# Second pair of PSUM banks for the odd node blocks at the end of a GNN layer, with task lists of their own

## The chip, the cores and the metric

The kernel runs on one core of a Trainium2 chip. The metric is the device time of one execution in microseconds; the kernel before took 619.28 us, the median of three runs (618.55 to 620.71).

## What is computed

One layer of a graph network over N = 50000 nodes and E = 25000 edges (sorted by destination), with rows of H = 128 floats, in fp32. The reference, cut:

```python
em = jnp.concatenate([x[src], x[dst]], axis=-1)
em = relu(layer_norm(em @ msg_w + msg_b, msg_g, msg_beta)) * edge_weights[:, None]
messages = segment_sum(em, dst) / (counts + 1e-08) * valid
gate = sigmoid(x @ gate_w + gate_b)
combined = jnp.concatenate([x, messages], axis=-1)
h_new = relu(layer_norm(combined @ upd_w + upd_b, upd_g, upd_beta))
out = layernorm(x + gate * h_new + (1.0 - gate) * x)
```

## The kernel before

**Tiling.** The edges come in 49 groups of 512 (four tiles of 128), the nodes in 98 blocks of 512, taken as 49 pairs k = 0 to 48; (k, 0) is the even and (k, 1) the odd block of a pair. P = 128, ROW = 129 (128 columns and one for the gate).

**Walk.** Each engine runs the same numbered steps: some written out, a loop, and from step 48 on written out again. Edge group g is worked on in step g, and the nodes follow a few steps behind it, since a block's messages must be stored first. Each engine has a list of tasks by hand; `node(task, at, lag, b)` runs a task for block (step - lag, b), and skips it where that pair doesn't exist; `edge` does the same for the groups. Engines are tied together by counting semaphores only, and each works its list strictly in order. After step 48 there are no edge groups left but the last `message_update` (L747) in step 49, so steps 49 to 52 (ACT: to 53) hold node tasks alone.

**A node block, in order of its data.** SP loads x_rows (L371) and the window of summed-up message rows (L389). PE transposes x into ps_x (`x_transposes`, L755) and ACT copies it to xT (`xT_of`, L555). DVE builds the one-hot matrix (`one_hots`, L1042). PE forms the sums u = x W + onehot messages in ps_u, two tiles at a time (`first_update`, `other_update`, L765 and L767). ACT takes their squares with row sums (`first_squares`, `other_squares`, L560), the gate (`gates`, L576), log and exp of the variance (`u_ln_of` L581, `u_rstd_of` L586), and then normalises out of ps_u into un (`first_norms`, `other_norms`, L593). PE transposes un into ps_t (`update_transposes`, L782), ACT applies scale, shift and relu (`hT_of`, L606), PE transposes back into ps_h (`back_transposes`, L789). DVE adds the residual (`residual`, L1056), takes statistics (`y_halves`, L1063) and some eight small operations (`sums`, L1073 to L1093), ACT gives log and exp of that variance (`y_ln_of` L611, `y_rstd_of` L616), and DVE writes the rows (`result`, L1108), which SP stores (L404).

**PSUM.** ps_xs and ps_xd are the banks of the edge transposes, ps_z that of the messages; ps_x, ps_t and ps_h one bank each. ps_u has two banks: tiles 0 and 1 of a block in one, 2 and 3 in the other, and every block uses the same two. So `update` waits until the block before has been normed out of the same bank:

```python
wait(pe, un_ready, k.at(4, 2 * b - 1 + a))
```

**The lists before, in the node steps.** With the lag and b in brackets, edge tasks left out. ACT: u_rstd(4,1), xT(3,0), norms(4,1), first squares(3,0), y_ln(5,1), hT(4,1), y_rstd(5,1), other squares(3,0), xT(3,1), gates(3,0), u_ln(3,0), u_rstd(3,0), norms(3,0), y_ln(4,0), y_rstd(4,0), hT(3,0), both squares(3,1), u_ln(3,1), gates(3,1). PE: back(4,0), first update(3,0), update transposes(4,1), other update(3,0), x transposes(3,1), back(4,1), first update(3,1), update transposes(3,0), other update(3,1), x transposes(2,0). DVE: residual(4,1), result(4,0), y_halves(4,1), one_hots(2,0), sums(4,1), residual(3,0), one_hots(2,1), result(4,1), y_halves(3,0), sums(3,0). ACT runs y_rstd of (s - 5, 1) in its step s, for the result that DVE has in its step s - 1. `sums` holds the small operations of the named y and also the first of the gate of the following block.

Of the kernel before, what the change touches and what calls it, by code (L numbers as in the profile page):

```python
# [7 lines left out]
ACT = mybir.ActivationFunctionType  # L8
AX = mybir.AxisListType
F32 = mybir.dt.float32  # L10
# [3 lines left out]
P = 128  # L14
# [12 lines left out]
ROW = P + 1  # L27
# [34 lines left out]
def gnn_kernel(nc, x, src, dst, edge_weight, msg_w, msg_b, msg_g, msg_beta,  # L62
# [8 lines left out]
    NK = NB // 2  # L71
# [10 lines left out]
    with ExitStack() as ctx:  # L82
        def sb(name, shape, dt=F32):
            return ctx.enter_context(nc.sbuf_tensor(name, shape, dt))

        def psum(name):
            return ctx.enter_context(nc.psum_tensor(name, [P, 512], F32))
# [17 lines left out]
        u_x_gate = sb("u_x_gate", [P, ROW])  # L105
# [14 lines left out]
        squares = sb("squares", [P, 3, 512])  # L120
# [10 lines left out]
        xT = [sb(f"xT{s}", [P, 512]) for s in range(2)]  # L131
        onehot = [sb(f"onehot{s}", [P, 512]) for s in range(2)]
# [3 lines left out]
        gate_exp = [sb(f"gate_exp{s}", [P, T]) for s in range(2)]  # L136
        gate_small = [sb(f"gate_small{s}", [P, 3, T]) for s in range(2)]
        un = [sb(f"un{s}", [P, 512]) for s in range(2)]
# [13 lines left out]
        node_recip = sb("node_recip", [P, 3, T])  # L152


        ps_xs = psum("ps_xs")
        ps_xd = psum("ps_xd")
        ps_z = psum("ps_z")
        ps_x = psum("ps_x")
        ps_t = psum("ps_t")
# [1 line left out]
        ps_u = ctx.enter_context(nc.psum_tensor("ps_u", [P, 1024], F32))  # L161
        ps_h = psum("ps_h")

        def sel_out(n):

            return (ps_h, ps_x, ps_t)[n // 3][:, n % 3 * ROW:(n % 3 + 1) * ROW]

        def u_tile(j, n):
            return ps_u[:, (j // 2) * 512 + (j % 2) * ROW:][:, 0:n]

        u_by_bank = ps_u[:].rearrange("p (a c) -> p a c", a=2)[:, :, 0:2 * ROW].rearrange(
            "p a (t h) -> p a t h", h=ROW)
        u_gates = u_by_bank[:, :, :, P:ROW]


        w_mean = sb("w_mean", [P, 4])
# [56 lines left out]
        def walk_sem(name):  # L233
            walk_sems.append(sem(name))
            return walk_sems[-1]
# [21 lines left out]
        hot_ready, un_ready, y_ready, y_var_ready, out_ready = (  # L257
            walk_sem("hot_ready"), walk_sem("un_ready"), walk_sem("y_ready"),
            walk_sem("y_var_ready"), walk_sem("out_ready"))
# [4 lines left out]
        def wait(eng, semaphore, value):  # L264

            if not (isinstance(value, int) and value <= 0):
                eng.wait_ge(semaphore, value)
# [4 lines left out]
        def walk(eng, step, last_lag, unroll=2):  # L272

            count = (NK - 1 - last_lag - 2) // unroll
            start = NK - 1 - unroll * count
            for c in range(start):
                step(Step(c))
            with eng.Fori(0, count) as m:
                for c in range(start, start + unroll):
                    step(Step(c, m, unroll))  # L280
            for c in range(NK - 1, NK + last_lag):
                step(Step(c))

        def edge(task, at, lag):
            g = at.back(lag)
            if g.inside(HEAD, EG):
                task(g)

        def node(task, at, lag, b):
            k = at.back(lag)  # L290
            if k.inside(0, NK):
                task(k, b)
# [30 lines left out]
        def _(sp):  # L323
# [129 lines left out]
            with is_general(sp):  # L453
                for s in range(2):
                    sp.wait_ge(rows_stored[s], 16)
                restart(sp, 1)
                all_edges(sp, store_rows)
                sum_by_node()
                restart(sp, 2)
                head()  # L460
                walk(sp, lambda at: step(at, by_window=False), 4)
            with sp.Else():
                walk(sp, step, 4)
# [43 lines left out]
        def _(act):  # L507
# [49 lines left out]
            def u_squares(k, b, a):  # L557
                act.wait_ge(u_done, k.at(4, 2 * b + a + 1))
                for j in (2 * a, 2 * a + 1):
                    last = nc.scalar.activation(squares[:, b, j * P:(j + 1) * P], u_tile(j, P), ACT.Square,  # L560
                                                accum_out=u_square[b][:, j:j + 1])
                if a == 1:
                    last.then_inc(u_square_ready, 1)
# [7 lines left out]
            def gates(k, b):  # L571
                act.wait_ge(u_done, k.at(4, 2 * b + 2))
                if k.m is None:

                    wait(act, gate_chain, k.at(4, 2 * b - 3))
                nc.scalar.activation(gate_exp[b][:].rearrange("p (a t) -> p a t", a=2).unsqueeze(3), u_gates,  # L576
                                     ACT.Exp, bias=gate_bias[:], scale=-1.0).then_inc(gate_exp_ready, 1)

            def u_ln_of(k, b):
# [8 lines left out]
            def u_norm(k, b, a):  # L588
                if a == 0:
                    act.wait_ge(u_rstd_ready, k.at(2, b + 1))  # L590
                    wait(act, un_in, k.at(2, b - 1))
                for j in (2 * a, 2 * a + 1):
                    last = nc.scalar.activation(un[b][:, j * P:(j + 1) * P], u_tile(j, P), ACT.Copy,  # L593
                                                scale=u_rstd[b][:, j:j + 1])
                last.then_inc(un_ready, 1)

# [31 lines left out]
                    whole_edge(Step(g))  # L628

            def step(at):  # L630
                node(u_rstd_of, at, 4, 1)
                node(xT_of, at, 3, 0)
                node(first_norms, at, 4, 1)
                node(other_norms, at, 4, 1)
                edge(xsT_of, at, 0)
                edge(xdT_of, at, 0)
                node(first_squares, at, 3, 0)
                node(y_ln_of, at, 5, 1)
                node(hT_of, at, 4, 1)
                node(y_rstd_of, at, 5, 1)  # L640
                node(other_squares, at, 3, 0)
                node(xT_of, at, 3, 1)
                node(gates, at, 3, 0)
                node(u_ln_of, at, 3, 0)
                node(u_rstd_of, at, 3, 0)
                node(first_norms, at, 3, 0)
                node(other_norms, at, 3, 0)
                edge(z_squares, at, 0)
                node(y_ln_of, at, 4, 0)
                edge(z_ln_of, at, 0)  # L650
                node(y_rstd_of, at, 4, 0)
                edge(z_rstd_of, at, 0)
                node(hT_of, at, 3, 0)
                node(first_squares, at, 3, 1)
                node(other_squares, at, 3, 1)
                edge(emT_of, at, 0)
                node(u_ln_of, at, 3, 1)
                node(gates, at, 3, 1)
# [14 lines left out]
        def _(pe):  # L673
            def tile(t, j):
                return t[:, j * P:(j + 1) * P]
# [15 lines left out]
            for n in range(2 * T):  # L691
                for c in range(2):
                    last = nc.tensor.matmul(sel_out(n), sel[:, c, n * P:(n + 1) * P], sel_rhs[:, c, :],
                                            start=c == 0, stop=c == 1)
# [63 lines left out]
            def update(k, b, a):  # L758
                slot = 2 * (k.c % 2) + b
                if a == 0:  # L760
                    pe.wait_ge(xT_ready, k.at(2, b + 1))
                    pe.wait_ge(hot_ready, k.at(2, b + 1))
                wait(pe, un_ready, k.at(4, 2 * b - 1 + a))
                for j in (2 * a, 2 * a + 1):
                    nc.tensor.matmul(u_tile(j, ROW), tile(xT[b], j), u_x_gate[:], start=True, stop=False,  # L765
                                     skip_group_check=True)
                    last = nc.tensor.matmul(u_tile(j, P), tile(onehot[b], j),  # L767
                                            window[slot][:, j * ROW:j * ROW + P], start=False, stop=True,
                                            skip_group_check=True)
                last.then_inc(u_done, 1)  # L770
# [48 lines left out]
                    message_update(g)  # L819

            def step(at):
                node(back_transposes, at, 4, 0)
                edge(dst_transposes, at, 0)
                edge(message_update, at, 1)
                edge(src_transposes, at, 0)
                node(first_update, at, 3, 0)
                node(update_transposes, at, 4, 1)
                node(other_update, at, 3, 0)
                node(x_transposes, at, 3, 1)
                edge(message, at, 0)  # L830
                node(back_transposes, at, 4, 1)
                node(first_update, at, 3, 1)
                node(update_transposes, at, 3, 0)
                node(other_update, at, 3, 1)
                node(x_transposes, at, 2, 0)
                edge(message_transposes, at, 0)
# [23 lines left out]
            with is_general(pe):  # L860
                restart(pe, 1)
                for c in range(2):
                    last = nc.tensor.transpose(ps_u[:, c * P:(c + 1) * P], weight_f[:, c, :], ident)
# [379 lines left out]
```

## Time and profile before

| what | value |
|---|---|
| median of 3 runs | 619.28 us (618.55 to 620.71) |
| the profiled execution | 617.63 us, its span 615.8 us |
| busy, share of the span | PE 89%, DVE 86%, ACT 86%, POOL 62% |
| granted TensorE clock, mean | 0.970 of 2.4 GHz |
| last edge work on PE (L747) | 572.08 us |
| last result of DVE begins | 611.94 us |

All times below are of the profiled execution, in us from the start of its span. A row of a timeline gives the start, the duration, the engine, line and operation, and, in brackets, how long the engine stood idle before it and what released it. Durations of one engine's rows can overlap a little: what an instruction takes of its engine is the distance to the next start.

### The profile page before, as it was taken

What the parts mean: (1) busy time and instruction counts of PE and PEld (TensorE: products, weight loads), DVE (VectorE), ACT (ScalarE), POOL (GpSimd) and SP (SyncE); (2) the same over time, 40 slices, a digit from 0 to 9 for tenths busy, and PEclk for the clock granted to TensorE, in tenths of its full rate; (3) what the DMA queues carried; (4) which work ended last, traced back from release to release, by engine and by line L of the source; (5) the groups of instructions that cost most, each with busy time, mean ns of one, the idle gap of its engine ahead of it and who ended that gap; (6) DMA issues with size and microseconds to landing.
All of it is one profiled execution on the core that took longest, in us unless ns stands there. A gap on an engine that the chain in (4) does not pass through costs nothing.

```text
span 615.8 us, 19234 instructions
## 1 busy us (share of the span) xinstructions
PE 546.9 (89%) x4552; PEld 522.8 (85%) x4600; DVE 532.2 (86%) x2434; ACT 531.7 (86%) x2500; POOL 382.5 (62%) x396
## 2 busy tenths in 40 slices
PE   1354799999999999999999999999999999999761
PEld 0353799999999999999999999999999999999660
DVE  4990159999989999999999999999999999999986
ACT  0021499999999999999999999999999999999883
POOL 0787777777777777777776767677676776300000
PEclk9985799999999999999999999999999999999996
DMA  3213468887878878788787877878778787756642
GB/s 108 70 43 91 134 177 212 208 228 203 225 214 212 221 201 229 209 210 224 199 227 200 219 209 212 224 190 225 211 211 220 198 227 198 205 156 169 173 116 69
DMA packets 192823, 115.12 MB, mean 187 GB/s; under 512 B 15053, under 2 KB 186390, under 8 KB 192790
## 3 DMA queue, kind: packets, MB, share of 16 engines
q1 hardware_dynamic: 178550, 88.63, 51.6%
q0 software_dynamic: 12544, 25.72, 18.2%
q10 hardware_dynamic: 1696, 0.40, 0.3%
q8 instruction: 13, 0.21, 0.1%
q14 instruction: 20, 0.16, 0.1%
HBM read 75.72 MB, written 38.97 MB: 186 GB/s over the span
## 4 chain that ended last, share of the span: by engine, by line
PE 70%; ACT 13%; DVE 9%; issue 5%; DMA 2%; SPq 1%; DVEq 0%; ACTq 0%
PE ps_u L765 12%; PE ps_u L767 11%; PE ps_z L747 8%; PE ps_z L732 7%; PE ps_z L734 6%; PE ps_t L782 5%; PE ps_h L789 5%; PE ps_x L755 5%; PE ps_xs L741 4%; ACT squares L560 3%; PE ps_xd L715 3%; PE ps_xs L715 3%; ACT un L593 3%; ACT squares L534 2%; ACT hT L606 1%
## 5 line engine op out<-in xcount | busy, mean ns | idle before, releaser
L471 POOL DMA_INDIRECT pair_rows<-in_x,gather_idx x392 | 382.3, 975 | 146.9 <-issue 112.6
L765 PE MATMUL ps_u<-u_x_gate,xT 128*128 128x129 f32 x784 | 155.2, 280 | 9.5 <-ACT un L593 9.2
L767 PE MATMUL ps_u<-window,onehot 128*128 128x128 f32 x784 | 151.2, 274 | 0.0
L765 PEld LDWEIGHTS ps_u<-u_x_gate,xT 128*128 128x128 f32 x784 | 118.5, 191 | 13.0 <-issue 6.4
L767 PEld LDWEIGHTS ps_u<-window,onehot 128*128 128x128 f32 x784 | 119.0, 192 | 0.0
L1108 DVE TENSOR_SCALAR out_rows<-y,y_small,y_rstd 128x128 f32<-128x128 f32 x392 | 111.6, 359 | 4.5 <-ACT y_rstd L616 4.5
L593 ACT ACTIVATE un<-ps_u,u_rstd 128x128 f32<-128x128 f32 x392 | 112.1, 373 | 3.2
L1056 DVE SCALAR_TENSOR_TENSOR y<-ps_h,gate_small,x_rows 128x128 f32<-128x128 f32 x392 | 109.9, 343 | 1.0 <-PE ps_h L789 1.0
L560 ACT ACTIVATE squares<-ps_u 128x128 f32<-128x128 f32 x392 | 107.6, 300 | 3.5 <-PE ps_u L767 3.3
L560 ACT ACTIVATION_READ_ACCUMULATOR squares<-ps_u 128x1 f32 x392 | 90.1, 232 | 0.0
L1063 DVE BATCH_NORM_STATS2 y_stats<-y 128x6 f32<-128x128 f32 x392 | 84.8, 280 | 0.0
L732 PE MATMUL ps_z<-weights,xsT 128*128 128x128 f32 x392 | 76.9, 278 | 4.6 <-ACT xsT L524 1.6
L606 ACT ACTIVATE hT<-ps_t,columns 128x512 f32<-128x512 f32 x98 | 77.7, 793 | 2.8 <-PE ps_t L782 2.7
L734 PE MATMUL ps_z<-weights,xdT 128*128 128x128 f32 x392 | 77.2, 279 | 0.0
L1042 DVE SCALAR_TENSOR_TENSOR onehot<-window,const_in 128x512 f32<-128x512 f32 x98 | 72.8, 743 | 4.1 <-DMA window<-rows_scratch 3.4
L732 PEld LDWEIGHTS ps_z<-weights,xsT 128*128 128x128 f32 x392 | 64.6, 195 | 1.9
L524 ACT COPY xsT<-ps_xs 128x512 f32<-128x512 f32 x49 | 29.8, 609 | 40.3 <-PE ps_xs L715 40.3
L534 ACT ACTIVATE squares<-ps_z 128x128 f32<-128x128 f32 x196 | 52.2, 304 | 11.1 <-PE ps_z L734 11.1
L747 PE MATMUL ps_z<-weights,emT 128*128 128x128 f32 x392 | 59.1, 296 | 2.7 <-ACT emT L549 2.4
L747 PEld LDWEIGHTS ps_z<-weights,emT 128*128 128x128 f32 x392 | 49.5, 198 | 13.4 <-ACT emT L549 12.4
L734 PEld LDWEIGHTS ps_z<-weights,xdT 128*128 128x128 f32 x392 | 60.8, 196 | 0.0
L782 PE MATMUL ps_t<-const_in,un 128*128 128x128 f32 x392 | 58.9, 273 | 2.0 <-ACT un L593 2.0
(133 smaller groups left out, 1023.3 us busy)
## 6 DMA issues: line engine op xcount, KB each, us to landing
x_rows<-in_x SPq DMA_DIRECT2D x98, 256.0 KB
out<-out_rows SPq DMA_DIRECT2D x98, 256.0 KB
window<-rows_scratch SPq DMA_DIRECT2D x196, 112.9 KB
rows_scratch<-msg_rows SPq DMA_DIRECT2D x49, 258.0 KB
pair_rows<-in_x,gather_idx POOLq DMA_INDIRECT x392
const_in<-in_constants SPq DMA_DIRECT2D x1, 954.0 KB, 5.3
rows_scratch<-pad_rows SPq DMA_DIRECT2D x5, 64.5 KB, 3.0
weights<-in_L_gnn_msg_w ACTq DMA_DIRECT2D x1, 128.0 KB, 5.2
```

The lines of the kernel that those rows point to most:

```text
L471: return nc.gpsimd.indirect_dma_start(rows[:, j * P:(j + 1) * P], None, x, bass.IndirectOffsetOnAxis(ap=offsets, axis=0))
L560: last = nc.scalar.activation(squares[:, b, j * P:(j + 1) * P], u_tile(j, P), ACT.Square, accum_out=u_square[b][:, j:j + 1])
L593: last = nc.scalar.activation(un[b][:, j * P:(j + 1) * P], u_tile(j, P), ACT.Copy, scale=u_rstd[b][:, j:j + 1])
L732: nc.tensor.matmul(tile(ps_z, j), tile(xsT[g.c % 2], j), w_src, start=False, stop=False, skip_group_check=True)
L734: last = nc.tensor.matmul(tile(ps_z, j), tile(xdT[g.c % 2], j), w_dst, start=False, stop=True, skip_group_check=True)
L747: last = nc.tensor.matmul(tile(ps_z, j), tile(emT[g.c % 2], j), u_msg, start=True, stop=True)
L765: nc.tensor.matmul(u_tile(j, ROW), tile(xT[b], j), u_x_gate[:], start=True, stop=False, skip_group_check=True)
L767: last = nc.tensor.matmul(u_tile(j, P), tile(onehot[b], j), window[slot][:, j * ROW:j * ROW + P], start=False, stop=True, skip_group_check ...
L782: last = nc.tensor.transpose(tile(ps_t, j), tile(un[b], j), ident)
L1056: last = v.scalar_tensor_tensor(y[b][:, cols], ps_h[:, cols], gates[:, 1, j:j + 1], x_rows[2 * (k.c % 2) + b][:, cols], ALU.mult, ALU.add)
L1063: last = v.bn_stats(y_stats[b][:, j], y[b][:, j * P:(j + 1) * P])
L1108: last = v.tensor_scalar(out_rows[b][:, cols], y[b][:, cols], y_small[b][:, 5, j:j + 1], y_rstd[b][:, j:j + 1], ALU.subtract, ALU.mult)
```

## The change

ps_xs and ps_xd become two halves of one tensor ps_e (the same two banks in all). In the pairs 46, 47 and 48 the odd block's sums go to ps_e instead of ps_u, and a block then waits for the norms of the block two before it, (46, 1) for none. From step 49 on ACT and PE follow new lists. DVE's, SP's and POOL's lists stay.

```diff
-        ps_xs = psum("ps_xs")
-        ps_xd = psum("ps_xd")
+        ps_e = ctx.enter_context(nc.psum_tensor("ps_e", [P, 1024], F32))
+        ps_xs, ps_xd = ps_e[:, 0:512], ps_e[:, 512:1024]
...
-        def u_tile(j, n):
-            return ps_u[:, (j // 2) * 512 + (j % 2) * ROW:][:, 0:n]
+        def after_edges(k):
+            return k.m is None and k.c >= NK - 3
+
+        def u_banks(k, b):
+            return ps_e if after_edges(k) and b == 1 else ps_u
+
+        def u_tile(k, b, j, n):
+            return u_banks(k, b)[:, (j // 2) * 512 + (j % 2) * ROW:][:, 0:n]
...
+        def all_in(at):
+
+            return at.m is None and at.c >= NK
...
             def step(at):
+                if all_in(at):
+                    node(u_rstd_of, at, 4, 1)
+                    node(first_norms, at, 4, 1)
+                    node(other_norms, at, 4, 1)
+                    node(xT_of, at, 3, 0)
+                    node(first_squares, at, 3, 0)
+                    node(other_squares, at, 3, 0)
+                    node(gates, at, 3, 0)
+                    node(u_ln_of, at, 3, 0)
+                    node(xT_of, at, 3, 1)
+                    node(u_rstd_of, at, 3, 0)
+                    node(hT_of, at, 4, 1)
+                    node(first_norms, at, 3, 0)
+                    node(other_norms, at, 3, 0)
+                    node(y_ln_of, at, 5, 1)
+                    node(y_rstd_of, at, 5, 1)
+                    node(first_squares, at, 3, 1)
+                    node(other_squares, at, 3, 1)
+                    node(hT_of, at, 3, 0)
+                    node(u_ln_of, at, 3, 1)
+                    node(gates, at, 3, 1)
+                    node(y_ln_of, at, 4, 0)
+                    node(y_rstd_of, at, 4, 0)
+                    return
...
-                wait(pe, un_ready, k.at(4, 2 * b - 1 + a))
+                if not after_edges(k) or (k.c, b) == (NK - 3, 0):
+                    wait(pe, un_ready, k.at(4, 2 * b - 1 + a))
+                elif k.c > NK - 3:
+
+                    wait(pe, un_ready, k.at(4, 2 * b - 3 + a))
...
             def step(at):
+                if all_in(at):
+                    node(back_transposes, at, 4, 0)
+                    edge(message_update, at, 1)
+                    node(first_update, at, 3, 0)
+                    node(other_update, at, 3, 0)
+                    node(x_transposes, at, 3, 1)
+                    node(update_transposes, at, 4, 1)
+                    node(first_update, at, 3, 1)
+                    node(other_update, at, 3, 1)
+                    node(back_transposes, at, 4, 1)
+                    node(x_transposes, at, 2, 0)
+                    node(update_transposes, at, 3, 0)
+                    return
```

The first `step` is ACT's, the second PE's; the readers of the sums (squares, gates, norms) take the banks from `u_banks` as well.

## Rows read from the trace of the kernel before

**Rows 1.** Windows: stretch, length, busy of PE, PEld, DVE, ACT, POOL; PEclk, DMA, GB/s

```profile
574.68:584.66 9.98, 6.67 (x58) 6.25 (x57) 9.98 (x51) 8.26 (x38) 0.00 (x0) 1.00 0.67 180
584.66:594.64 9.98, 6.66 (x58) 6.25 (x57) 8.88 (x45) 8.27 (x38) 0.00 (x0) 1.00 0.55 151
```

**Rows 2.** Who waited for whom, 571 to 616 us: us, times, longest

```profile
PE ps_u L765 <- ACT un L593: 8.5, 6, 1.7
...
DVE out_rows L1108 <- ACT y_rstd L616: 4.5, 4, 1.6
```

**Rows 3.** Timeline of PE: start us, us, what, [idle before <- releaser]

```profile
578.45 0.46 PE L765 MATMUL ps_u<-u_x_gate,xT 128*128 128x129 f32 x2 [1.60 <-ACT un L593]
...
579.42 0.60 PE L782 MATMUL ps_t<-const_in,un 128*128 128x128 f32 x4
...
580.75 0.60 PE L755 MATMUL ps_x<-const_in,x_rows 128*128 128x128 f32 x4
581.19 0.60 PE L789 MATMUL ps_h<-const_in,hT 128*128 128x128 f32 x4
```

**Rows 4.** Timeline of ACT, same columns

```profile
572.17 0.20 ACT L586 ACTIVATE u_rstd<-u_ln 128x4 f32<-128x4 f32 x1
572.27 0.58 ACT L555 COPY xT<-ps_x 128x512 f32<-128x512 f32 x1
572.73 1.16 ACT L593 ACTIVATE un<-ps_u,u_rstd 128x128 f32<-128x128 f32 x4
574.68 0.28 ACT L560 ACTIVATE squares<-ps_u 128x128 f32<-128x128 f32 x1 [0.80 <-PE ps_u L767]
...
575.29 0.78 ACT L606 ACTIVATE hT<-ps_t,columns 128x512 f32<-128x512 f32 x1
575.96 0.21 ACT L616 ACTIVATE y_rstd<-y_ln 128x4 f32<-128x4 f32 x1
576.05 0.28 ACT L560 ACTIVATE squares<-ps_u 128x128 f32<-128x128 f32 x1
...
577.17 0.24 ACT L581 ACTIVATE u_ln<-u_square 128x4 f32<-128x4 f32 x1
577.45 0.20 ACT L586 ACTIVATE u_rstd<-u_ln 128x4 f32<-128x4 f32 x1
577.68 1.14 ACT L593 ACTIVATE un<-ps_u,u_rstd 128x128 f32<-128x128 f32 x4
```

**Rows 5.** Timeline of DVE, same columns

```profile
576.41 1.11 DVE L1108 TENSOR_SCALAR out_rows<-y,y_small,y_rstd 128x128 f32<-128x128 f32 x4
...
579.04 1.12 DVE L1056 SCALAR_TENSOR_TENSOR y<-ps_h,gate_small,x_rows 128x128 f32<-128x128 f32 x4
...
581.88 0.73 DVE L1042 SCALAR_TENSOR_TENSOR onehot<-window,const_in 128x512 f32<-128x512 f32 x1
...
586.17 1.12 DVE L1108 TENSOR_SCALAR out_rows<-y,y_small,y_rstd 128x128 f32<-128x128 f32 x4 [1.10 <-ACT y_rstd L616]
...
596.15 1.11 DVE L1108 TENSOR_SCALAR out_rows<-y,y_small,y_rstd 128x128 f32<-128x128 f32 x4 [1.31 <-ACT y_rstd L616]
...
605.13 1.12 DVE L1108 TENSOR_SCALAR out_rows<-y,y_small,y_rstd 128x128 f32<-128x128 f32 x4 [1.56 <-ACT y_rstd L616]
```

**Rows 6.** Timeline of PE, 64 to 65 us and its last two groups

```profile
64.53 0.63 PE L732 MATMUL ps_z<-weights,xsT 128*128 128x128 f32 x2 [1.59 <-ACT xsT L524]
64.95 0.63 PE L734 MATMUL ps_z<-weights,xdT 128*128 128x128 f32 x2
...
603.53 0.66 PE L782 MATMUL ps_t<-const_in,un 128*128 128x128 f32 x4 [2.03 <-ACT un L593]
605.06 0.66 PE L789 MATMUL ps_h<-const_in,hT 128*128 128x128 f32 x4 [0.87 <-ACT hT L606]
```

**Rows 7.** Windows around the last work of PE, columns as in rows 1

```profile
604.00:606.00 2.00, 0.85 (x6) 0.42 (x4) 0.87 (x4) 0.87 (x2) 0.00 (x0) 1.00 0.00 0
606.00:607.00 1.00, 0.00 (x0) 0.00 (x0) 1.00 (x6) 0.00 (x0) 0.00 (x0) 0.71 0.00 0
```

More of the change, by code:

```diff
@@ L166, in sel_out, with u_gates @@
             return (ps_h, ps_x, ps_t)[n // 3][:, n % 3 * ROW:(n % 3 + 1) * ROW]
-        def u_tile(j, n):
-            return ps_u[:, (j // 2) * 512 + (j % 2) * ROW:][:, 0:n]
-        u_by_bank = ps_u[:].rearrange("p (a c) -> p a c", a=2)[:, :, 0:2 * ROW].rearrange(
-            "p a (t h) -> p a t h", h=ROW)
-        u_gates = u_by_bank[:, :, :, P:ROW]
+        def after_edges(k):
[4 more added lines that the diff above has]
+            return u_banks(k, b)[:, (j // 2) * 512 + (j % 2) * ROW:][:, 0:n]
+        def u_gates(k, b):
+            return u_banks(k, b)[:].rearrange("p (a c) -> p a c", a=2)[:, :, 0:2 * ROW].rearrange(
+                "p a (t h) -> p a t h", h=ROW)[:, :, :, P:ROW]
         w_mean = sb("w_mean", [P, 4])
@@ L559, in u_squares @@
                 for j in (2 * a, 2 * a + 1):
-                    last = nc.scalar.activation(squares[:, b, j * P:(j + 1) * P], u_tile(j, P), ACT.Square,
+                    last = nc.scalar.activation(squares[:, b, j * P:(j + 1) * P], u_tile(k, b, j, P), ACT.Square,
                                                 accum_out=u_square[b][:, j:j + 1])
@@ L575, in gates @@
                     wait(act, gate_chain, k.at(4, 2 * b - 3))
-                nc.scalar.activation(gate_exp[b][:].rearrange("p (a t) -> p a t", a=2).unsqueeze(3), u_gates,
+                nc.scalar.activation(gate_exp[b][:].rearrange("p (a t) -> p a t", a=2).unsqueeze(3), u_gates(k, b),
                                      ACT.Exp, bias=gate_bias[:], scale=-1.0).then_inc(gate_exp_ready, 1)
@@ L592, in u_norm @@
                 for j in (2 * a, 2 * a + 1):
-                    last = nc.scalar.activation(un[b][:, j * P:(j + 1) * P], u_tile(j, P), ACT.Copy,
+                    last = nc.scalar.activation(un[b][:, j * P:(j + 1) * P], u_tile(k, b, j, P), ACT.Copy,
                                                 scale=u_rstd[b][:, j:j + 1])
@@ L762, in update @@
                     pe.wait_ge(hot_ready, k.at(2, b + 1))
-                wait(pe, un_ready, k.at(4, 2 * b - 1 + a))
+                if not after_edges(k) or (k.c, b) == (NK - 3, 0):
+                    wait(pe, un_ready, k.at(4, 2 * b - 1 + a))
+                elif k.c > NK - 3:
+                    wait(pe, un_ready, k.at(4, 2 * b - 3 + a))
                 for j in (2 * a, 2 * a + 1):
-                    nc.tensor.matmul(u_tile(j, ROW), tile(xT[b], j), u_x_gate[:], start=True, stop=False,
+                    nc.tensor.matmul(u_tile(k, b, j, ROW), tile(xT[b], j), u_x_gate[:], start=True, stop=False,
                                      skip_group_check=True)
-                    last = nc.tensor.matmul(u_tile(j, P), tile(onehot[b], j),
+                    last = nc.tensor.matmul(u_tile(k, b, j, P), tile(onehot[b], j),
                                             window[slot][:, j * ROW:j * ROW + P], start=False, stop=True,
```

## The prediction

> **What bounds the kernel now.** I read the busy time by stretch first, then the waits of the end, then the timelines of the three engines that share it. Nothing before the last edge group is touched, so all of the change lies after about 572 us, where three steps with node blocks 46, 47 and 48 (a pair each) and a draining step remain. [Rows 1] show two of those steps, 9.98 us each: PE works 6.7 us, ACT 8.3, DVE 10.0 and 8.9. No engine is plainly full, and the trace says why. PE waits six times for the norms L593 that read ps_u, 8.5 us together, and DVE waits for y_rstd L616 four times, 4.5 us together [rows 2]. The loop is short: a block's sums can't begin in ps_u before the block ahead of it has been normed out of it. In [rows 3] PE stands 1.60 us at L765 until 578.45; ACT's norms of the same moment began at 577.68 [rows 4]. The second chain is the one that matters most below. DVE runs strictly in its written order: result(44,1), y_halves, small sums, residual, result(45,0), y_halves, one_hots(47,0), and so on. In [rows 5] result(44,1) starts at 576.41 and one_hots(47,0) at 581.88, 5.47 us later with DVE never idle; result(45,1) starts at 586.17, after 1.10 us of waiting for y_rstd.
>
> **The change part by part.** Banks: for blocks (46,1), (47,1), (48,1) the sums go to the banks of the edge transposes. The instructions are the same in number, shape and length; only the wait falls back by two blocks. That takes away PE's 1.60 us gap, six of them or 8.5 us of PE time [rows 2]. This is no time of the kernel by itself: what it is worth depends on DVE, whose own waits in the last steps are 1.10, 1.31 and 1.56 us [rows 5], 3.97 in sum. No banks can give more than that, as long as DVE does the same work.
>
> Orders: no instruction is added. SP's and POOL's lists are untouched, and so is DVE's. What moves is where ACT issues y_ln and y_rstd of lag 5. Before, they come after the first squares: y_rstd(44,1) runs at 575.96, right behind hT [rows 4], and DVE's result(44,1) starts when it is through with the work ahead, at 576.41 [rows 5]. In the new list they stand behind both squares, gates, xT, u_rstd, hT and all four norms of block (46,0). I schedule that step from the rows. ACT does u_rstd(45,1) at 572.17 as before; its norms follow 0.24 later (577.45 to 577.68 in [rows 4] is 0.23) at 572.41 and take 1.01 (four of 0.25), so xT(46,0), now behind them, starts at 573.42 instead of 572.27. Its row lasts 0.58, so PE begins the sums of (46,0) at 574.03. Half a block of sums takes 0.90: from 579.42 to 580.75 in [rows 3] lie four transposes and such a half, 1.33, and four transposes take 0.44 (580.75 to 581.19). Both halves now run in a row, until 575.83, and ACT reads the second one 0.2 later, as a group's row of 0.60 ends 0.16 behind the 0.44 to the next. From 576.03 ACT issues: squares 0.50 (574.68 to 575.29 in [rows 4] is a pair with y_ln), gates 0.13, u_ln at 576.70 when the squares' sums are through, xT(46,1), u_rstd at 577.27, hT(45,1) 0.66 (575.29 to 575.96), norms(46,0) from 578.03 to 579.04, y_ln(44,1) and 0.24 later y_rstd(44,1) at 579.28. DVE's result(44,1) starts 0.24 after that: 579.52, not 576.41. **That is 3.1 us late in the first of the steps**, and DVE has nothing else it may do in the meantime.
>
> Behind the waiting result are queued y_halves, the small sums, residual, result(45,0) and one_hots(47,0). PE needs the one-hots for the sums of (47,0), so the delay comes round: result(44,1) 579.52, one_hots(47,0) 5.47 later at 584.99, through 0.80 later (row 0.73 plus the signal), sums of (47,0) at 585.79. From the start of the sums to result(45,1) lie the same tasks as in the first step, 574.03 to 579.52, 5.49. So result(45,1) starts at 591.28 against 586.17, and the loop has a period of 5.47 + 0.80 + 5.49 = 11.76 us against 9.98 (586.17 to 596.15 in [rows 5]). result(46,1) comes at 603.04 against 596.15, 6.9 late. In the last stretch DVE doesn't wait any more for what it waited for before: the gap of 1.65 between the end of the residual and 605.13 (1.56 by the row) is filled, because the y_rstd of (47,1) comes out while DVE is still behind. 6.9 - 1.65 = 5.25: **the lists cost 5.3 us at the full clock.** The end behind the last result (the store) is as before.
>
> The loads lie beside this. The window of 47 is issued after the store of result(44,1), and one_hots(47,0) comes the same 5.47 after that result in both; x_rows move with the residual. Both shift with the delay and cost nothing; if that cover were gone, a row load would have to be late by over 3 us to show. The new wait of the gates (on the small sums two blocks back) is met. It falls near in step 50, some tenths.
>
> The clock: the trace of before holds the full one through gaps of 1.60 us with PE busy 6.7 of 9.98 [rows 1, 3]. It shows it falling from 2.4 to 1.2 GHz once in the end: PE had finished at 601.50, ran two groups of 0.66 after 2.03 and 0.87 us of idleness [rows 6], and the granted clock goes from 1.00 to 0.71 in the window from 606 [rows 7]. In the new steps PE is emptier than that: between the transposes of un(46,0), done at 580.6, and the sums of (47,0) at 585.79 it has four transposes of 0.44 to do, in 5.2 us. I take it that the clock falls there, in each of two steps. At the lower level two rows of matmuls start 0.42 apart, 64.53 to 64.95 [rows 6], against 0.22, so a half costs 0.85 more and both 1.7; both are on the loop (the second squares wait for the second half). With a tenth for the transposes behind them that is 1.8 for each of the steps of 47 and 48: 3.6. Bounds: 0 if the clock holds, 5.4 if it also holds back the first step or the last four groups. Sum: 5.3 + 3.6 = 8.9 us.
>
> The profiled execution took 617.63 (span 615.8), which gives 626.5; the median of the runs is 1.65 above it, 619.28, which gives **628.2**.
>
> A rule that speaks against me: the Trainium skill (Perfetto Trace Analysis, Identifying the Most-Contended Engine) says that the same gap repeating on an engine can mean too few PSUM buffers. By that the 1.6 us gaps should go and the steps shorten; the trace has the repeating gap, and rival B prices what its going would give.
>
> **The rivals.** (A) The lists cost what I worked out but the clock stays at 2.4 GHz, since single groups of transposes are enough to keep it. Then the time is 619.28 + 5.3 = 624.6. For it: the clock held until 606 with two short groups after 601.5. Against: it then fell. (B) Faster, by one mechanism: the second pair of banks frees PE, and y_rstd(44,1) reaches DVE by 576.41 all the same. DVE then loses none of 1.10, 1.31 and 1.56 us: 619.28 - 4.0 = 615.3. Its place is the first result of lag 4 after the last edges, and it decides at 576.41. For it: the bank wait is the longest in the end [rows 2]. Against: ACT is a list in order, and between 576.03 and the norms' end stand 3 us of work in front of it. (C) The new lists cost and give about the same: if PE's early sums let ACT reach the norms 3 us sooner, result(44,1) would be on time and the rest as before, 619.3. That would need xT(46,0) earlier, and it is moved later by 1.1. That the change does nothing can't be: both lists apply from step 49 on.
>
> **How the numbers follow.** The forecast with the fall of the clock has 0.62, A 0.24, B 0.06, C 0.04, and 0.04 goes to something slower than 631. The range holds the forecast and A: from 624.0 (A less its tenths) to 630.5 (5.3 + 5.4 = 10.7, and half a microsecond for signals). A measurement of this kernel can tell about 0.3%, 1.9 us, from no change. Slower by more: 0.90; within: 0.04; faster: 0.06.
>
> **What would show it.** DVE's out_rows L1108 should wait for y_rstd about 3 us in each of three steps, and no longer at the end; two starts of result(k,1) should lie 11.8 us apart, or 13.5 with the clock down; PE's wait for un L593 should be nearly gone, in its place L765 waiting for the one-hots by about 2 us and L789 for the residual by 2 to 3; PEclk below 1 in the stretches from about 584 to 588 and 598 to 602. Wrong would be: result(44,1) starting before 578, or steps of under 10 us.

## The result and the profile after

The changed kernel takes 628.2 us, the median of four runs (627.7 to 628.7); the kernel before took 618.9 beside it. The ratio is 1.015, with a 95% interval of 1.012 to 1.018: slower by 1.5%. The forecast was 628.2, its range 624.0 to 630.5. The profiled execution took 628.65, with a span of 626.8. The page of the changed kernel:

```profile
span 626.8 us, 19234 instructions
...
PE 552.5 (88%) x4552; PEld 528.0 (84%) x4600; DVE 532.1 (85%) x2434; ACT 531.8 (85%) x2500; POOL 382.0 (61%) x396
...
PEclk9995699999999999999999999999999999999885
```

The instructions are as many as before, 19234, and PE has 552.5 us busy against 546.9: the same matmuls, some at the lower clock.

The spans of the two profiled executions differ by 11.0 us, but not all of that is the change. The last group of L747 (L782 in the changed file) begins at 572.08 us before and at 574.37 after, although nothing ahead of it was edited. Over all the profiled executions of this study it begins between 571.7 and 575.8. So from here on I count the **end**: from the start of that last edge group on PE to the start of the last result on DVE. It is 39.86 us before (572.08 to 611.94) and 48.59 after (574.37 to 622.96), **8.7 us more**. The medians of the two kernels differ by 9.3 us.

The waits of the end, of the changed kernel (who waited for whom, us in total, times, the longest), which answer to [rows 2]:

```profile
DVE out_rows L1160 <- ACT y_rstd L627: 13.3, 4, 4.8
ACT squares L571 <- PE ps_u L806: 10.4, 6, 3.5
PE ps_h L828 <- DVE y L1108: 10.1, 4, 3.1
...
PE ps_u L804 <- issue: 3.6, 2, 1.8
```

PE's 8.5 us of waiting for the norms are gone from the list. DVE's wait for y_rstd has grown from 4.5 us to 13.3, and new ones stand behind it. The timeline of DVE, to be read beside [rows 5]:

```profile
581.96 1.11 DVE L1160 TENSOR_SCALAR out_rows<-y,y_small,y_rstd 128x128 f32<-128x128 f32 x4 [3.18 <-ACT y_rstd L627]
...
587.43 0.73 DVE L1094 SCALAR_TENSOR_TENSOR onehot<-window,const_in 128x512 f32<-128x512 f32 x1
...
595.34 1.11 DVE L1160 TENSOR_SCALAR out_rows<-y,y_small,y_rstd 128x128 f32<-128x128 f32 x4 [4.72 <-ACT y_rstd L627]
...
608.85 1.11 DVE L1160 TENSOR_SCALAR out_rows<-y,y_small,y_rstd 128x128 f32<-128x128 f32 x4 [4.85 <-ACT y_rstd L627]
```

result(44,1) comes 7.59 us after the start of the end (4.33 before), having waited 3.18 us. one_hots(47,0) follows 5.47 us later, as before, and the next two results of (k,1), with k = 45 and 46, come 13.38 and 13.51 us apart, where before it was 9.76 and 9.98. They wait 4.72 and 4.85 us. After that DVE doesn't wait until the last result, for which it stands 0.51 us as before. ACT in the first of the steps, beside [rows 4]:

```profile
575.70 0.60 ACT L566 COPY xT<-ps_x 128x512 f32<-128x512 f32 x1
...
578.44 0.28 ACT L571 ACTIVATE squares<-ps_u 128x128 f32<-128x128 f32 x1 [0.27 <-PE ps_u L806]
...
580.44 1.15 ACT L604 ACTIVATE un<-ps_u,u_rstd 128x128 f32<-128x128 f32 x4
581.44 0.25 ACT L622 ACTIVATE y_ln<-y_small 128x4 f32<-128x4 f32 x1
581.72 0.20 ACT L627 ACTIVATE y_rstd<-y_ln 128x4 f32<-128x4 f32 x1
```

The order is the one laid out ahead: the copy to xT(46,0) behind the norms, the second pair of squares at 578.44, norms(46,0) at 580.44, and y_ln and y_rstd(44,1) only behind them. PE in the same stretch, beside [rows 3]:

```profile
576.35 0.49 PE L804 MATMUL ps_u<-u_x_gate,xT 128*128 128x129 f32 x2 [0.83 <-ACT xT L566]
...
582.60 0.60 PE L821 MATMUL ps_t<-const_in,un 128*128 128x128 f32 x4
585.85 0.63 PE L828 MATMUL ps_h<-const_in,hT 128*128 128x128 f32 x4 [2.65 <-DVE y L1108]
588.26 0.77 PE L804 MATMUL ps_u<-u_x_gate,xT 128*128 128x129 f32 x2 [1.78 <-issue]
588.83 0.64 PE L806 MATMUL ps_u<-window,onehot 128*128 128x128 f32 x2
589.25 0.64 PE L804 MATMUL ps_u<-u_x_gate,xT 128*128 128x129 f32 x2
```

PE has the four back transposes at 585.85 and otherwise nothing from 583.2 to 588.26. For the idle time ahead of 588.26 the trace names no releaser (`issue`); one_hots(47,0) ends at 588.16 (587.43 and its 0.73), 0.1 us ahead, and these sums read it. Then the rows of the sums of (47,0) start 0.42 to 0.44 us apart instead of 0.22. That is the granted clock, in windows of the changed kernel (columns as in [rows 1]):

```profile
583.00:588.00 5.00, 0.83 (x6) 0.42 (x4) 5.00 (x27) 3.16 (x11) 0.00 (x0) 1.00 0.75 194
588.00:591.00 3.00, 2.74 (x13) 2.77 (x14) 2.62 (x15) 0.63 (x4) 0.00 (x0) 0.50 0.33 99
596.00:601.00 5.00, 1.21 (x10) 0.77 (x8) 5.00 (x28) 3.50 (x14) 0.00 (x0) 1.00 0.66 174
```

It is at 1.00 while PE works 0.83 of 5 us, and has fallen to 0.50, which is 1.2 GHz, when the sums come. The same happens a step later, after 596 to 601. Both halves of the sums take 3.36 us from their first start to that of the x transposes behind them (588.26 to 591.62), where in the first step, at 1.00, they took 1.89 (576.35 to 578.24).

### The profile page after: what moved, and what is told of

Same layout as the page of the kernel before. It is cut to its first block, busy times and chain, and to the rows that moved or that the text cites. A ratio compares the mean times of both kernels' runs of the same rounds, so it can differ in the third digit from the quotient of the medians.

```text
span 626.8 us, 19234 instructions
## 1 busy us (share of the span) xinstructions
PE 552.5 (88%) x4552; PEld 528.0 (84%) x4600; DVE 532.1 (85%) x2434; ACT 531.8 (85%) x2500; POOL 382.0 (61%) x396
## 4 chain that ended last, share of the span: by engine, by line
PE 71%; DVE 10%; ACT 10%; issue 5%; DMA 2%; SPq 1%; DVEq 0%; ACTq 0%
PE ps_u L804 12%; PE ps_u L806 11%; PE ps_z L782 8%; PE ps_z L767 7%; PE ps_e L750 6%; PE ps_z L769 6%; PE ps_h L828 5%; PE ps_t L821 5%; PE ps_x L790 5%; PE ps_e L776 4%; ACT un L604 2%; ACT squares L571 2%; DVE out_rows L1160 2%; DVE y L1108 2%; ACT squares L545 1%
## 5 line engine op out<-in xcount | busy, mean ns | idle before, releaser
L804 PE MATMUL ps_u<-u_x_gate,xT 128*128 128x129 f32 x760 | 152.5, 283 | 5.6 <-issue 3.6
L806 PE MATMUL ps_u<-window,onehot 128*128 128x128 f32 x760 | 148.3, 277 | 0.0
L804 PEld LDWEIGHTS ps_u<-u_x_gate,xT 128*128 128x128 f32 x760 | 116.9, 194 | 8.6 <-issue 5.0
L1160 DVE TENSOR_SCALAR out_rows<-y,y_small,y_rstd 128x128 f32<-128x128 f32 x392 | 110.8, 357 | 13.3 <-ACT y_rstd L627 13.3
L806 PEld LDWEIGHTS ps_u<-window,onehot 128*128 128x128 f32 x760 | 117.3, 195 | 0.0
L571 ACT ACTIVATE squares<-ps_u 128x128 f32<-128x128 f32 x380 | 104.3, 300 | 11.8 <-PE ps_u L806 11.8
L604 ACT ACTIVATE un<-ps_u,u_rstd 128x128 f32<-128x128 f32 x380 | 108.7, 374 | 3.1
L571 ACT ACTIVATION_READ_ACCUMULATOR squares<-ps_u 128x1 f32 x380 | 87.2, 232 | 0.0
L828 PE MATMUL ps_h<-const_in,hT 128*128 128x128 f32 x392 | 60.3, 277 | 10.1 <-DVE y L1108 10.1
L750 PE MATMUL ps_e<-const_in,pair_rows 128*128 128x128 f32 x392 | 60.3, 279 | 5.4 <-issue 5.4
L535 ACT COPY xsT<-ps_e 128x512 f32<-128x512 f32 x49 | 29.8, 609 | 40.0 <-PE ps_e L750 40.0
L782 PE MATMUL ps_z<-weights,emT 128*128 128x128 f32 x392 | 58.5, 294 | 2.7 <-ACT emT L560 2.4
```

The lines of the kernel that those rows point to most:

```text
L750: last = nc.tensor.transpose(tile(bank, j), tile(rows[s], side * T + j), ident)
L782: last = nc.tensor.matmul(tile(ps_z, j), tile(emT[g.c % 2], j), u_msg, start=True, stop=True)
L804: nc.tensor.matmul(u_tile(k, b, j, ROW), tile(xT[b], j), u_x_gate[:], start=True, stop=False, skip_group_check=True)
L806: last = nc.tensor.matmul(u_tile(k, b, j, P), tile(onehot[b], j), window[slot][:, j * ROW:j * ROW + P], start=False, stop=True, skip_group ...
L828: last = nc.tensor.transpose(tile(ps_h, j), tile(hT[b], j), ident)
L1160: last = v.tensor_scalar(out_rows[b][:, cols], y[b][:, cols], y_small[b][:, 5, j:j + 1], y_rstd[b][:, j:j + 1], ALU.subtract, ALU.mult)
```

## Experiments

The end of each kernel's one profiled execution, counted as above, beside the median of 2 to 12 runs (two for experiments 7 and 8). The time of the kernel before is the one measured on the same chip with that batch.

| kernel | end, us | us, median | before, us | ratio (95%) |
|---|---|---|---|---|
| before | 39.86 | | | |
| changed | 48.59 | 628.2 | 618.9 | 1.015 (1.012 to 1.018) |
| 1 banks only | 37.58 | 617.1 | 619.7 | 0.996 (0.994 to 0.998) |
| 2 lists only | 50.46 | 629.2 | 619.7 | 1.017 (1.013 to 1.021) |
| 3 changed, y_rstd early | 44.40 | 624.7 | 619.7 | 1.009 (1.006 to 1.012) |
| 4 changed, clock held | 45.49 | 624.7 | 619.7 | 1.009 (1.006 to 1.012) |
| 5 banks, two moves on ACT | 35.92 | 616.4 | 620.4 | 0.994 (0.992 to 0.997) |
| 6 the two moves, no banks | 38.26 | 619.5 | 620.4 | 0.999 (0.997 to 1.000) |
| 7 banks, ACT's list | 50.05 | 630.4 | 620.4 | 1.016 (1.012 to 1.019) |
| 8 banks, PE's list | 48.80 | 629.8 | 620.4 | 1.015 (1.011 to 1.018) |
| 9 as 8, clock held | 43.38 | 622.9 | 620.1 | 1.007 (1.004 to 1.010) |
| 10 before, with filler | 40.34 | 618.6 | 620.1 | 0.999 (0.997 to 1.002) |

**1. The banks alone.** Both `if all_in(at):` branches are taken out of the changed kernel, so that ACT and PE follow the lists of before.

```diff
-                if all_in(at):
-                    node(u_rstd_of, at, 4, 1)
...
-                    return
```

> The second pair of banks stays, the task lists of before come back on ACT and PE. Theory 1 (the lists make y_rstd late and let the clock fall; the banks by themselves give a little): laid out with the durations of the rows, the last result starts 2.0 us earlier than in the kernel before, 37.9 us after the last edge matmuls begin against 39.9; 617 us; PEclk 1.00 until the drain; DVE's waits for y_rstd get no longer than 1.6 us each. Rival (the banks cost: sums written to the transposes' banks, or PE running ahead, slow the rest): 622 us or more, with most of the 8.7 us lost in it.

The end is 37.58 us, 2.28 below that of the kernel before, and the time 0.4% lower. The banks don't cost; they give. DVE's results of (k,1), and the waits:

```profile
587.61 1.11 DVE L1123 TENSOR_SCALAR out_rows<-y,y_small,y_rstd 128x128 f32<-128x128 f32 x4 [0.33 <-ACT y_rstd L627]
...
596.59 1.11 DVE L1123 TENSOR_SCALAR out_rows<-y,y_small,y_rstd 128x128 f32<-128x128 f32 x4 [0.33 <-ACT y_rstd L627]
...
605.08 1.11 DVE L1123 TENSOR_SCALAR out_rows<-y,y_small,y_rstd 128x128 f32<-128x128 f32 x4 [1.09 <-ACT y_rstd L627]
```

```profile
PE ps_t L797 <- ACT un L604: 3.6, 4, 2.0
...
PE ps_u L780 <- ACT xT L566: 2.6, 2, 1.4
DVE out_rows L1123 <- ACT y_rstd L627: 2.3, 4, 1.1
...
PE ps_u L780 <- ACT un L604: 0.3, 1, 0.3
```

DVE still waits 0.33, 0.33 and 1.09 us for a y_rstd where it waited 1.10, 1.31 and 1.56. Of PE's 8.5 us of waiting for the norms ahead of its sums 0.3 are left, but most of it comes back in other places: PE now waits for xT and for the norms that the update transposes need. Experiment 5 shows that this does no harm: PE's waits are nearly the same there (3.3 us for the norms and 2.1 for xT at ps_u), and DVE has almost none.

**2. The lists alone.** All sums go to ps_u, with the wait of before.

```diff
-            return ps_e if after_edges(k) and b == 1 else ps_u
+            return ps_u
...
-                if not after_edges(k) or (k.c, b) == (NK - 3, 0):
-                    wait(pe, un_ready, k.at(4, 2 * b - 1 + a))
-                elif k.c > NK - 3:
-
-                    wait(pe, un_ready, k.at(4, 2 * b - 3 + a))
+                wait(pe, un_ready, k.at(4, 2 * b - 1 + a))
```

> The new lists stay, all sums go to ps_u again with its wait of before. Theory 1: the result of lag 4 waits about 3 us and more for y_rstd as in the changed kernel, the clock falls, the last result starts 47 to 50 us after the last edge matmuls begin (before 39.9, changed 48.6): 626 to 629 us. Rival (the banks cost): back to about 619 us.

The end is 50.46, a little above the range I gave. Without the banks the lists are 1.9 us worse than with them. The first result of (k,1) waits 3.18 us, exactly as in the changed kernel, and the waits in all are:

```profile
DVE out_rows L1156 <- ACT y_rstd L627: 14.9, 6, 5.3
...
PE ps_u L800 <- ACT un L604: 4.9, 3, 1.9
PE ps_u L800 <- DVE onehot L1090: 4.3, 2, 2.2
```

So the loss is the lists', and the banks take some of it back.

**3. y_rstd early.** One move in ACT's new list.

```diff
                     node(first_squares, at, 3, 0)
+                    node(y_ln_of, at, 5, 1)
+                    node(y_rstd_of, at, 5, 1)
                     node(other_squares, at, 3, 0)
...
                     node(other_norms, at, 3, 0)
-                    node(y_ln_of, at, 5, 1)
-                    node(y_rstd_of, at, 5, 1)
```

> The changed kernel, with y_ln and y_rstd of lag 5 moved on ACT from behind the norms of (k,0) to between its two pairs of squares, nothing else. If the late y_rstd is the whole loss of the lists: near or below the kernel before, 615 to 619 us. My layout by the rows says less: result(44,1) is on time, but then the residual waits 0.8 us for back transposes, which the PE list holds behind both sums of (k,1), and result(45,0) waits 1.3 us for a y_rstd behind hT and gates: 2.1 us over before at the full clock (621), up to 5 with the clock down (624). No change from 628 would say that y_rstd is not it.

4.2 us come back, to 44.40, and not 8.7. result(44,1) is now on time, 4.33 us into the end as before. What waits next is what the layout had named, the residual for the back transposes and results for a y_rstd further down:

```profile
DVE y L1108 <- PE ps_h L828: 4.5, 3, 1.9
DVE out_rows L1160 <- ACT y_rstd L627: 4.2, 5, 1.1
```

The clock still falls to 0.50 in two stretches, around 586 to 589 and 596 to 599, so this run doesn't tell how the 4.5 us that stay over the kernel before divide between these waits and the clock.

**4. The clock held.** The changed kernel, with transposes of a constant whose result isn't read. They add to what is computed and change nothing of it.

```diff
+            def filler(n):
+                pe.wait_ge(rows_ready, EG)
+                for j in range(n):
+                    nc.tensor.transpose(tile(ps_z, j % T), ident, ident)
...
                     node(back_transposes, at, 4, 0)
+                    if NK < at.c < NK + 3:
+                        filler(10)
...
                     node(update_transposes, at, 3, 0)
+                    if at.c < NK + 2:
+                        filler(16)
                     return
```

> The changed kernel with transposes of a constant into ps_z, whose result nobody reads: 16 behind the update transposes of (k,0), 10 behind the back transposes of (k,0), in PE's gaps of 2.65 and 1.78 us. If the fall of the clock is worth 3.5 us, as I have it: PEclk 1.00 through the steps, starts of result(k,1) 11.8 us apart instead of 13.4, 624.7 us. Rival (the clock is off the loop and the 13.4 come from waits alone): 628 us or more.

On PE the filler stands in the two gaps, and the sums follow at full pace:

```profile
580.84 1.91 PE L820 MATMUL ps_z<-const_in 128*128 128x128 f32 x16
...
584.12 1.25 PE L820 MATMUL ps_z<-const_in 128*128 128x128 f32 x10
586.07 0.46 PE L804 MATMUL ps_u<-u_x_gate,xT 128*128 128x129 f32 x2 [0.69 <-issue]
```

```profile
583.00:588.00 5.00, 3.65 (x31) 3.48 (x32) 5.00 (x25) 2.25 (x9) 0.00 (x0) 1.00 0.69 187
```

PE is busy 3.65 of 5 us in the stretch where it was 0.83, and the granted clock is 1.00 in every window of 1 us from the start of the end until the drain. DVE's results of (k,1):

```profile
579.76 1.11 DVE L1169 TENSOR_SCALAR out_rows<-y,y_small,y_rstd 128x128 f32<-128x128 f32 x4 [3.20 <-ACT y_rstd L627]
...
591.65 1.11 DVE L1169 TENSOR_SCALAR out_rows<-y,y_small,y_rstd 128x128 f32<-128x128 f32 x4 [3.23 <-ACT y_rstd L627]
...
603.54 1.11 DVE L1169 TENSOR_SCALAR out_rows<-y,y_small,y_rstd 128x128 f32<-128x128 f32 x4 [3.23 <-ACT y_rstd L627]
```

They lie 11.89 us apart, for 11.76 laid out, and the end is 45.49 us: 3.1 below the changed kernel. The first result is where it was (7.60 us into the end, 7.59 in the changed kernel), and from result(46,1), the third of these, to the last result both take 14.11 us; all of the 3.1 lies in the two steps in which the clock had fallen. The changed kernel's last groups on PE, at 1.2 GHz too (rows of 1.09 and 1.06 us), cost nothing. **The fall of the clock was worth 3.1 us, and the whole change at the full clock 5.6.**

**5. Banks and two moves on ACT.** PE's list is that of before, and so is ACT's but for this, from step 49 on:

```diff
                     node(y_ln_of, at, 5, 1)
+                    node(y_rstd_of, at, 5, 1)
                     node(hT_of, at, 4, 1)
-                    node(y_rstd_of, at, 5, 1)
...
+                    node(first_squares, at, 3, 1)
                     node(hT_of, at, 3, 0)
-                    node(first_squares, at, 3, 1)
```

> Banks of the change, PE's list of before, ACT's list of before with two moves from step 49 on: y_rstd of lag 5 from behind hT of (k-1,1) to ahead of it, and the first squares of (k,1) ahead of hT of (k,0). Theory 1 (with the banks only y_rstd behind hT holds DVE back, 0.33, 0.33 and 1.09 us in the run with the banks alone): DVE has no wait over 0.1 us until the very last one, last result 36.2 us after the last edge matmuls begin (before 39.9, banks alone 37.6): 3.7 us below the kernel before, about 616. Rival (the wait moves to the residual, as hT is now later): 37.5 us or more, 617.

The end is 35.92 us, and this is the fastest version: 0.6% below the kernel before, where the banks alone gave 0.4%. The three results of (k,1):

```profile
586.58 1.12 DVE L1147 TENSOR_SCALAR out_rows<-y,y_small,y_rstd 128x128 f32<-128x128 f32 x4
...
595.22 1.12 DVE L1147 TENSOR_SCALAR out_rows<-y,y_small,y_rstd 128x128 f32<-128x128 f32 x4
...
602.79 1.11 DVE L1147 TENSOR_SCALAR out_rows<-y,y_small,y_rstd 128x128 f32<-128x128 f32 x4 [0.17 <-ACT y_rstd L627]
```

Between the first two DVE has no wait, and they lie 8.64 us apart, which is what DVE's own work takes. Only 0.17 us are left at the third, where I had expected none over 0.1. DVE is the bound now: while its own list stays, a better order on ACT or PE could give it these 0.17 us and part of the 0.51 that it waits for the very last result.

**6. The two moves without the banks.** ACT's list is that of experiment 5, the sums are those of experiment 2.

> ACT's list with the two moves, PE's list of before, all sums in ps_u with its wait of before. Theory 1: PE's wait for the norms stays and only DVE's wait behind hT goes: last result 38.3 us after the last edge matmuls, 1.6 below the kernel before, 618. Were the order of ACT all that counts, it would be equal to the run with banks and moves, 36.2.

38.26, as laid out. DVE keeps waits of 0.43, 1.17 and 0.66 us:

```profile
587.12 1.11 DVE L1143 TENSOR_SCALAR out_rows<-y,y_small,y_rstd 128x128 f32<-128x128 f32 x4 [0.43 <-ACT y_rstd L627]
...
596.95 1.11 DVE L1143 TENSOR_SCALAR out_rows<-y,y_small,y_rstd 128x128 f32<-128x128 f32 x4 [1.17 <-ACT y_rstd L627]
...
605.01 1.11 DVE L1143 TENSOR_SCALAR out_rows<-y,y_small,y_rstd 128x128 f32<-128x128 f32 x4 [0.66 <-ACT y_rstd L627]
```

So the two moves give 1.6 us without the banks and 1.7 with them (37.58 to 35.92), and the banks 2.3 either way. These are differences between single profiled executions. In the medians the 1.6 us doesn't stand out: 619.5 against 620.4, with an interval that reaches to 1.000. In experiment 6 the clock had also fallen ahead of the last two groups on PE.

**7. ACT's new list alone.** The `all_in` branch is taken out on PE only.

> Banks and ACT's new list, PE's list of before. If ACT's list alone makes the loss: result of lag 4 waits about 3 us each step, and my layout gives 47.0 us from the last edge matmuls to the last result at the full clock, 48 to 50 with the clock down; about 628. If the two lists need each other's order and PE's is the culprit: near 40, 619.

The end is 50.05 us, 1.5 more than with both lists. DVE's waits for y_rstd are 3.62, 5.30 and 5.28 us; the second:

```profile
596.58 1.11 DVE L1147 TENSOR_SCALAR out_rows<-y,y_small,y_rstd 128x128 f32<-128x128 f32 x4 [5.30 <-ACT y_rstd L627]
```

The clock falls twice before the drain, around 589 to 592 and 603 to 606. ACT's list is enough for the whole loss.

**8. PE's new list alone.** The branch is taken out on ACT only.

> Banks and PE's new list, ACT's list of before. y_rstd of lag 5 is early again, but both sums of (k,1) stand ahead of the back transposes of (k-1,1) and both of (k,0) ahead of the update transposes: by my layout 3.3 us over the kernel before at the full clock, 43.2 us, up to 4 with the clock down; about 623. If ACT's list alone makes the loss: 38 to 40 us, 617 to 619.

This missed: 48.80 us where I had 43.2. PE's list makes the whole loss by itself as well. The granted clock, and the waits:

```profile
589.00:594.00 5.00, 3.04 (x28) 2.81 (x27) 3.48 (x13) 3.69 (x19) 0.00 (x0) 1.00 0.18 54
...
594.00:597.00 3.00, 3.00 (x19) 3.00 (x18) 1.25 (x12) 1.24 (x6) 0.00 (x0) 0.60 0.85 210
601.00:604.00 3.00, 2.91 (x15) 2.92 (x16) 1.70 (x6) 1.80 (x10) 0.00 (x0) 0.57 0.03 7
608.00:611.00 3.00, 3.00 (x17) 3.00 (x17) 1.31 (x12) 1.61 (x7) 0.00 (x0) 0.54 0.29 87
```

```profile
ACT hT L617 <- PE ps_t L797: 12.0, 7, 3.0
DVE out_rows L1136 <- ACT y_rstd L627: 8.1, 5, 3.9
```

The clock falls three times before the drain. The last three windows take in the falls and what follows them, and PE is full there since the same matmuls take longer. In the 5 us up to 594, just ahead of the first fall, PE works 3.04 us, and its longest gap there is 1.96. The kernel before kept the full clock with 3.33 of 5 (583 to 588) and gaps of 1.6 to 1.7. So here it fell with PE a good deal busier than the 0.83 of 5 us in the changed kernel. The new wait is hT's for the update transposes, 12 us, which in PE's list come after both halves of the sums and the x transposes; with the clock held, in experiment 9, it is 7.2.

**9. The same, clock held.** Experiment 8 with the filler of experiment 4, in other gaps (`filler(9)` after the back transposes of (k,0), 14 after the update transposes of (k-1,1), 6 after those of (k,0)).

> The run with the banks and PE's new list only, and transposes of a constant into ps_z put into PE's gaps: 14 behind the update transposes of (k-1,1), 6 behind those of (k,0), 9 behind the back transposes of (k-1,0). That run missed my 43.2 us by 5.6. If the fallen clock is what I left out (it was 1.2 GHz in three stretches, and PE's list is in the loop all the time): 43.5 to 45 us from the last edge matmuls to the last result, 11 us a step. If waits that my layout doesn't have are the cause: 48 us or more still.

43.38 us, a little below the range I gave, with the clock at 1.00 until the drain. The layout was right for the waits (3.3 laid out, 3.5 measured) and had the clock too small, up to 4 us where it is 5.4 of the 48.8. The two runs agree until it falls: the second result of (k,1) comes 16.38 us into the end in both, the third 30.79 in experiment 8 and 27.48 here. Two of DVE's results of (k,1), 11.1 us apart:

```profile
589.78 1.12 DVE L1147 TENSOR_SCALAR out_rows<-y,y_small,y_rstd 128x128 f32<-128x128 f32 x4 [1.52 <-ACT y_rstd L627]
...
600.88 1.12 DVE L1147 TENSOR_SCALAR out_rows<-y,y_small,y_rstd 128x128 f32<-128x128 f32 x4 [1.52 <-ACT y_rstd L627]
```

**10. A control.** The kernel before with 8 transposes of the filler ahead of each first update from (46,1) to (48,1).

> A control: the kernel before, with 8 such transposes ahead of each first update in the last steps, in gaps of 1.6 to 1.7 us. The clock is at 1.00 there anyway. If the added transposes cost and give nothing by themselves: 39.9 us from the last edge matmuls to the last result, ratio 1.000. If they delay PE: over 40.5.

DVE's results start within 0.03 us of where they do in the kernel before, for the first six (4.33 to 27.77 us into the end). The end is 40.34, not 39.9: the last two groups of PE, of 0.66 us in [rows 6], took 1.10 and 1.12 here, since the clock had fallen before them and not after. The time is that of the kernel before, 0.999. So where the clock stands at 1.00 the filler neither costs nor gives, and what it gave in 4 and 9 is the clock. Whether the earlier fall at the drain has to do with the filler isn't shown; experiment 6, without any, has it there too.

## Why the prediction was right

**The late y_rstd.** Laid out: result(44,1) 3.1 us late. Measured: a wait of 3.18 and a start 7.59 us into the end instead of 4.33, 3.26 late. In experiment 3 this delay goes with a single move, and 4.2 us with it.

**The loop.** Laid out: 11.76 us from result to result at the full clock. Measured with the clock held: 11.89 and 11.89. The part through DVE is 5.47 in both.

**What comes back in the last stretch.** The wait of 1.56 us at result(47,1) is gone, as said: from result(46,1) to the last result lie 14.11 us, 15.79 before.

**The change at the full clock** was put at 5.3 and measured as 5.6 (45.49 against 39.86). Two loops of 0.13 more each and a first step of some 0.15 more make the difference.

**The clock** was put at 3.6, 1.8 in each of two steps, and measured as 3.1. The steps grew from 11.89 to 13.38 and 13.51, by 1.5 and 1.6: the last rows of the sums ran at the higher clock already (591.40 to 591.62, 0.22 apart again), so it was not the 1.7 of two full halves. (The rows at 64.53 in [rows 6], which the price was taken from, do lie at a granted clock of 0.50.) The fall came a little later than laid out, just as the sums began: some 13.6 us into the end (588), where 11.9 was laid out (584). The two errors nearly cancel: 5.6 + 3.1 = 8.7 for 8.9.

**That the median came out at 628.2 to the tenth is luck.** The start of the last edge group moves by 4 us from one execution to another, and the median of the kernel before was 618.9 to 620.4 in the four batches.

**The rivals.** A (the clock holds) was wrong, with 45.49 us as what it would have been. C (result(44,1) on time) was wrong by 3.26 us: xT(46,0) came later, as laid out. B (the banks free PE, and y_rstd is there in time) isn't what this change does, but it was right as a mechanism: with ACT's and PE's own lists kept, the banks gave 2.3 us, and with two moves 3.9, next to the 4.0 that I named as the most that DVE's waits hold. The rule of the Trainium skill that stood beside it is in the section Optimization Strategy of Perfetto Trace Analysis, and it speaks of the engine that should be saturated: the same gap repeating there can mean too few buffers. Experiment 1 agrees in part: with more banks PE's waits for the norms ahead of its sums went from 8.5 us to 0.3. But PE wasn't the engine that should be full, and the end got only 2.3 us shorter.

**What I had wrong.** The prediction laid the whole loss on ACT's list and gave PE's list no term of its own. Experiment 8 shows that PE's is as bad: 3.5 us of waits (43.38 against 39.86) and 5.4 of clock. With either list new, the loss is 9 to 10 us, and with both 8.7. They don't add. That each makes DVE wait on the same loop would explain it, but no run here was made to show it.

## What to carry to other kernels

When a buffer is doubled, leave the order of the tasks alone first and measure that. A list that puts the freed engine's own work first can hold back a tiny operation, here a y_rstd of 0.2 us, on which the engine that is really full waits once in every step. To price a new order, follow it round once from the full engine back to itself, with starts taken from the timeline: the period of that loop is the step. Then look at how empty PE gets in it, because a second loss sits there.

## What was not expected of the hardware

The clock did harm of the same order as the waits: 3.1 us beside 5.6 in the changed kernel, 5.4 beside 3.5 in experiment 8. With PE busy 0.83 of 5 us it fell to 1.2 GHz, and the sums behind it, on the loop, took 3.36 us instead of 1.89. In experiment 8 it first fell after 5 us in which PE had worked 3.04. 52 transposes that nobody needs, 26 for each of two steps, brought back the 3.1 us, and the same kind cost nothing where the clock was up (experiment 10).

In the kernel before the clock fell at 606 us, after the last group on PE, in experiments 1 and 5 it had fallen before that last group, and in experiments 6 and 10 before the last two, in 10 with the same gap of 2.0 us ahead of them as before. When exactly it falls differs from run to run, and so does, by up to 4 us, the time that the unchanged part ahead takes. The length of time at 1.2 GHz doesn't explain the second. Added up from windows of 1 us, the part ahead has 27.3 us at the lower clock in eight of the twelve profiled executions, all of it in the first 100 us, and among these eight the last edge group begins between 571.66 and 575.81. Where the 4 us come from stays open.
